# Recurrence steps of a 48-channel scan on one NeuronCore: the products taken by kind over both batches, and both rough sums ahead of both states

## The reference

```
def f(carry, inp):
    nxt = inp + _conv1d(carry, w, b)     # 48 -> 48 channels, 5 taps, padding 2
    return (nxt, nxt)
_, d_rest = jax.lax.scan(step(down_w, down_b), d0, xs[1:])
...  # the same for up (weights of down), right and left, each on the result of the one before
```

## Time and profile before

| | us |
|---|---|
| median of three runs | 10971.82 |
| the profiled execution | 10969.64 |
| its span | 10967.6 |
| TensorE busy (matmuls) | 9458.1 (86%) |
| VectorE busy | 8150.0 (74%) |
| ScalarE busy | 6288.6 (57%) |
| GpSimd busy | 2852.5 (26%) |

### The profile page before, as it was taken

How to read it: one execution, slowest core, us unless ns; L and a number is a source line. 1 busy time by engine, 2 the same in 40 slices (tenths; PEclk the granted TensorE clock), 3 DMA queues, 4 the chain that set the end, 5 groups by cost and what they waited for, 6 DMA issues and landing times. The chain is left out here.

```text
span 10967.6 us, 213297 instructions
## 1 busy us (share of the span) xinstructions
PE 9458.1 (86%) x72742; PEld 9064.4 (83%) x72742; DVE 8150.0 (74%) x16260; ACT 6288.6 (57%) x11049; POOL 2852.5 (26%) x4106
## 2 busy tenths in 40 slices
PE   0799999999999998989969997999799997999200
PEld 0799999999999997767759997999799997999200
DVE  7777777777777776878867776777699996777333
ACT  0577777767777774434446666999733335666200
POOL 0000000000000000000046665666466664666100
PEclk9999999999999998999989998999899998999655
DMA  8566666666666666989968886777666666787899
GB/s 357 119 132 130 132 132 129 133 119 133 131 130 134 132 131 135 260 221 257 249 127 199 199 200 164 214 205 206 174 195 213 213 201 171 193 198 195 312 432 409
DMA packets 727620, 2115.87 MB, mean 193 GB/s; under 512 B 57872, under 2 KB 632048, under 8 KB 636064
## 3 DMA queue, kind: packets, MB, share of 16 engines
q1 hardware_dynamic: 623712, 1913.29, 68.7%
q10 hardware_dynamic: 103808, 201.34, 5.8%
HBM read 1359.44 MB, written 754.97 MB: 193 GB/s over the span
## 5 line engine op out<-in xcount | busy, mean ns | idle before, releaser
L476 PE MATMUL conv_ps<-tap_high,x_high 128*128 128x432 f32 (+2 forms) x6144 | 1879.8, 306 | 43.7 <-DVE x_edge L552 29.7
L476 PE MATMUL conv_ps<-tap_low,x_high 128*128 128x432 f32 (+2 forms) x6144 | 1907.2, 310 | 0.0
L476 PE MATMUL conv_ps<-tap_high,x_low 128*128 128x432 f32 (+2 forms) x6144 | 1906.9, 310 | 0.0
L1221 POOL MEMSET down_u_in<- 32x8192 f32 x2 | 13.8, 6918 | 5199.8 <-POOLq L948 5199.8
L356 ACT ACTIVATE x_high<-raw,negmean 128x512 fp32r<-128x512 f32 x1024 | 1216.6, 1248 | 60.5 <-DMA raw_edge<-x 48.9
L548 DVE SCALAR_TENSOR_TENSOR x_low<-raw,negmean,x_high 128x512 fp32r<-128x512 f32 x1024 | 1148.1, 1151 | 120.3 <-ACT x_high L356 120.3
L476 PEld LDWEIGHTS conv_ps<-tap_high,x_high 128*128 128x128 f32 x6144 | 1161.9, 189 | 65.2 <-DVE x_edge L552 31.3
L476 PEld LDWEIGHTS conv_ps<-tap_low,x_high 128*128 128x128 f32 x6144 | 1163.0, 189 | 20.8 <-issue 0.2
L476 PEld LDWEIGHTS conv_ps<-tap_high,x_low 128*128 128x128 f32 x6144 | 1165.5, 190 | 17.3
L393 ACT COPY qk<-conv_ps 128x288 f32<-128x288 f32 x1024 | 414.4, 405 | 965.6 <-PE conv_ps L482 964.3
L563 DVE TENSOR_TENSOR qk<-conv_ps,qk 128x192 f32<-128x192 f32 x1024 | 366.9, 358 | 807.7 <-ACT vt L394 796.0
(11 more groups left out here) (191 smaller groups left out, 25423.2 us busy)
## 6 DMA issues: line engine op xcount, KB each, us to landing
raw<-x SPq DMA_DIRECT2D x764, 256.0 KB, 5.5
d_rows<-down_o_t SPq DMA_DIRECT2D x32, 3584.0 KB, 29.6
u_cols<-up_o_t SPq DMA_DIRECT2D x64, 1792.0 KB, 14.7
right_u_in<-u_cols SPq DMA_DIRECT2D x32, 3584.0 KB, 16.8
r_cols<-right_o_t SPq DMA_DIRECT2D x32, 3584.0 KB, 24.5
left_u_in<-r_cols SPq DMA_DIRECT2D x32, 3584.0 KB, 16.7
up_u_in<-d_rows SPq DMA_DIRECT2D x31, 3360.0 KB, 15.6
xs<-x SPq DMA_DIRECT2D x24, 4096.0 KB, 13.9
```

The lines of the kernel that those rows point to most:

```text
L476: nc.tensor.matmul(bank(dy, side, lo - side, hi - side), xs[at], ws[taps], start=fresh[side], stop=False, skip_group_check=True)
L1221: nc.gpsimd.memset(u_in[32:64, s], 0.0).then_inc(between_clear, 1)
```

## The change

Two lines are added, both `for b in range(B):`, so that one loop over the batches becomes three on TensorE and two on VectorE. No instruction, wait or semaphore count is added or removed; ScalarE, GpSimd and SyncE are unchanged.

```diff
@@ TensorE, in steps
                         for b in range(B):
                             pe.wait_ge(hi_ready[b], states0 + T * g + k)
                             ...  # three matmuls C, L1132
                             last.then_inc(conv_done[b], 1)
 
+                        for b in range(B):
                             pe.wait_ge(state_done[b], states0 + T * g + k)
                             ...  # three matmuls T, L1139
 
+                        for b in range(B):
                             pe.wait_ge(lo_ready[b], states0 + T * g + k)
                             ...  # three matmuls L, L1145
```

## The result

| | us |
|---|---|
| before, median of 4 runs | 10971.39 (10962.13 to 10974.5) |
| changed, median of 4 runs | 11227.34 (11222.25 to 11239.99) |
| ratio | 1.0236, 95% interval 1.0219 to 1.0254 |
| forecast | 11250 (11110 to 11340) |

The profiled execution has a span of 11225.6 us against 10967.6, 258.0 more. First the starts of S in the changed kernel, as in the earlier trace rows (S now stands at L1205).

What follows compares the result with a forecast made beforehand. TensorE's issue of 18 matmuls bounds down and nearly right; waits for ring room add in up and left. Longer steps add 204 us (down, right, left) and 76 (up), 280 on 10969.64: 11250 us, range 11110 to 11340.

Steps and rivals of the forecast that it cites:

- TensorE alone sets down and right, the ring's waits add in up and left: Before: TensorE's 18 matmuls make down's 2.141 us step, nearly right's; waits for ring room add 0.07 (up), 0.05 (left).
- C and T cost nothing outside up: Moving C and T forward on TensorE stays hidden: cast 1 has 0.4 us of cover, 0.07 in right.
- L1 waits for the second lo, every second step, 0.3 us, 2.83 + 1.76 us: TensorE stands 0.3 us before L1 every second step; two-step cycle 4.59 us, 2.295 per step in down, right, left.
- The slow pair counts, not the mean: GpSimd's lo alternates 0.64 and 0.74 us by step; the slow parity sets the cycle, the fast one (4.39) has slack.
- rival A: GpSimd's lo durations are mixed, not bound to step parity: mean pair 1.34, 2.245 us per step, about 11150 us; chance 0.16.
- The pair overlaps (1.44) and is not 1.50: On GpSimd the slow pair of lo takes 1.44 us; 1.50 would give 2.325 per step, 61 us more.
- rival B: GpSimd's pair of lo is slower than 1.44 us: 11311 us at 1.50, 11350 at 1.54; chance 0.12.
- 0.77 from L0's load to S0: Low chain: from TensorE's L0 weight load to VectorE's S0 takes 0.77 us, a member of the 2.83 us sum.
- Up at 9.44 us per four steps: Up: chain through casts, copies, ring and low chain takes 9.44 us, 2.36 per step against 2.211, adding 76 us.
- Left loses its waits for room: Left: the 126 waits of R0 for ScalarE's copy (68.0 us) go, as the copy now ends before R0 can start.
- Rival C: L1's load is met in time, TensorE issues without a stop, left falls to 2.141: about 10937 us; chance 0.06.
- Rival D: TensorE's clock drops to 1.2 GHz now and then: 400 us if in a tenth of steps, 11650 us; chance 0.02.

Runs made afterwards that it cites:

- e9: Kernel before with a ring of 16 lines instead of 8, and VectorE's awaited count of copied blocks lowered by two: 10907.73 us.
- e2: Changed kernel with four instead of two spare columns in each buffer of hi: 11060.37 us, ratio to before 1.0079.
- e3: Changed kernel with lo computed for half of the columns only, all instructions remaining: 10978.01 us, ratio to before 1.0007.
- e12: Changed kernel with four spare columns in hi, R1 also waiting for batch 0's rough_ready, and a ring of 16 lines: 10974.01 us.
- e6: Changed kernel with four spare columns in hi and R1 also waiting for batch 0's rough_ready: 11003.20 us, ratio to before 1.0038.
- e10: Kernel before with four instead of two spare columns in each buffer of hi: 10965.91 us, ratio to before 1.0003.
- e1: Changed kernel with S's two waits swapped, rough_ready first, then low_done: 11237.18 us, ratio to before 1.0244.
- e5: Changed kernel with one more wait ahead of R1, for rough_ready of batch 0: 11169.81 us, ratio to before 1.0187.

## Why the prediction was right, step by step

- *TensorE alone sets down and right, the ring's waits add in up and left.* Right: e9 brought up and left to within 0.005 of down's 2.141.
- *C and T cost nothing outside up.* Right: beyond the first step neither waited in down, right or left after the change.
- *L1 waits for the second lo, every second step, 0.3 us, 2.83 + 1.76 us.* Right to 0.01 in right and left, where the cycle of 4.60 is shown above. In up the sign given, some 250 waits of 0.3 us, came by half: of 246 only 122 are over 0.15 us, as its own sum over four steps has L1's wait once; e2 and e3 move the time with the length of lo as the cycle says.
- *The slow pair counts, not the mean.* Right; rival A would have had 2.245. e2 shows that the parity is the place of `hi`'s buffer.
- *The pair overlaps (1.44) and is not 1.50.* Right: 1.45 at 8502.14, and rival B falls. This agrees with the rule that the prediction took from the Trainium skill (GPSIMD Engine Reference, 2.1 Instruction dispatch).
- *0.77 from L0's load to S0.* Right in right, left and up (0.76). In down it was mis-sized: the prediction took the value of single rows, and 136 of the 256 slow steps have 0.67, so down is 2.269 and not 2.295. That is 0.026 x 511 = 13 us of the 23 by which 11250 is too high; about 6 us more is that the rest of the kernel ran that much shorter in the profiled execution.
- *Up at 9.44 us per four steps.* Right: 2.358 per step is 9.43, and the members are found in the timeline, so this is not luck. The member through the ring's wait is there (126 waits), and taking it out (e12 against e6) gave 0.051 per step.
- *Left loses its waits for room.* Right: none in the page after.
- Rival C (faster): its point was two lo in 1.11 us. e3's pair is two of 0.44, below that, and its time is that of the kernel before; left fell to 2.136, as C had it. But C left up as it was, and e3 has 2.300 there, so C's 10937 would have been some 40 us too low even with a short lo.
- Rival D (clock): it did not come. The granted clock stays at 1.00 in all four stretches after the change, with a standstill of TensorE's loads in every second step of down, right and left.
- Rival A would have had lo waits in every step, and rival E no change; neither came.

## What to carry to other kernels

When several chains share engines, compare chains and not only busy shares: GpSimd was busy 59% of down and still set the pace, because grouping by kind makes both batches ask for it at once. Follow the cycle through two steps, add what each member waits for, and take the slow member of a pattern that alternates, not the mean. Keep the batches half a step apart where one engine is at its limit, and give a ring more lines when the writer waits for room in it.

## What the runs showed of the hardware

- A GpSimd subtraction on 112 x 256 elements took 0.64 us in all steps with buffers of 260 columns apart and 0.64 or 0.74 in turn with 258 apart (e2, e10; one of 0.80 in right of each).
- Two such instructions back to back took 1.23 us, 0.04 less than twice one.
- On half of the columns the same instruction took 0.44 us in the median, not 0.32 (e3).
- Of two waits in front of a VectorE instruction, the late one cost 0.07 us more when it was written second (e1: 0.74 from load to S0, e5: 0.67), and 0.09 more when the other one's count was worked out in between (0.76). An additional wait that moved this work forward saved 0.49% of the time.
- A TensorE group whose first weight load had waited let the next group's load start 0.33 us later instead of 0.357.
